# A layer's last additions moved into the scatters: the residual stored to the output early, each expert block's rows added there by DMA

## The chip, the cores and the metric

The kernel runs on one core of one Trainium2 chip. The metric is the time of one execution on the device, in microseconds (us). The kernel before took 378.92 us as the median of 3 runs (378.6 to 380.24). One execution of it was also taken by the hardware profiler; all durations below come from that one.

## The reference

The input is x, 2048 tokens of 128 numbers, float32. Two stages, each with a residual:

```python
x = x + attention(layernorm(x))        # linear "cosformer" attention, 16 heads of 64, then Wo and bo
x = x + moe(layernorm(x))              # mixture of experts, below

logits = xf @ gate_w                   # 8 experts
top_w, top_idx = top_k(logits, 2)      # two experts for each token
top_w = softmax(top_w)
h = gelu(einsum('td,edf->tef', xf, w1) + b1)      # 128 -> 512, exact gelu
y = einsum('tef,efd->ted', h, w2) + b2            # 512 -> 128
out = einsum('ted,te->td', y, combine)            # the two chosen experts' rows, weighed and added
```

So each row of the output is the residual after attention plus two weighed expert results.

## The kernel before

The tokens are worked through in four stages of 512 (`NS = 4`, each of `SC = 4` tiles of 128). In the attention part TensorE (PE) has nearly all of the time. While stage i is in attention, the tokens of stage i-1 are normalised, gated and sent, twice each (once for each of their two experts), by GpSimd's indirect DMAs (`rows_out`) into `ybuf`, a table in DRAM that is sorted by expert. A row of `ybuf` holds the 128 normalised numbers, then a word with the place where the result is to go (column D, copied from `ids`), then the weight (column D + 1). Places that no token took hold 0xFFFF as their word, which is over the scatter's bound, so that such a row is skipped.

The mixture is then computed in `NB = 39` blocks of 128 rows of `ybuf`, each of one expert. A table `tab` says of each block its expert and where it begins. Its first 17 entries are known when three stages are routed (blocks that are already full, sorted by expert), the other 22 at the end (again sorted by expert; entries that are left over point at an empty block). The blocks run as a pipeline over the engines, in this order in each engine's own program:

- SyncE (SP), `load_block(b)`: reads the table, loads the rows into `yb` (a ring of 10) and the expert's first matrix into `w1b` (a ring of 6). From block 10 on it first waits until the scatter of block b-10 has landed (`z_out`), since the scatter reads its row numbers from `yb`.
- PE: transposes the rows (L1324), multiplies by w1 (`hidden`, L1337), then by w2 (`down`, L1352). ScalarE does the gelu (L638).
- VectorE (DVE), `weighed(b)`: adds the bias (`zs`, L986) and multiplies by the weights (`z`, L990, a ring of 8). From block 8 on it waits before L990 until the scatter of block b-8 has landed.
- GpSimd (POOL), `results_out(b)`: one indirect DMA writes the block's 128 rows to `zbuf` (L511). `zbuf` has 2 x 2048 rows, one half for each of a token's two experts, so that no two scatters ever write the same row and none waits for another. The scatters of blocks 0 to 13 are issued in an order written out by hand (`RESULTS_AT`): blocks 0 and 1 after `z` of block 2, block 2 after that of block 3, then four `rows_out`, blocks 3 and 4 after `z` of block 7, block 5 after block 8, 6 and 7 after 9, 8 after 10, 9 and 10 after 11, 11 after 12, and 12 and 13 after 13. From block 14 each waits for its own `z`.

When all 39 scatters have landed, SP and ScalarE's queue load both halves of `zbuf` back (`zin`, eight transfers of 256 KB), DVE adds them to the residual in `x_sb` (`add_results`, L997 and L999), and four stores write the output.

Of the kernel before, what the change touches and what calls it, by code (L numbers as in the profile page):

```python
# [36 lines left out]
SC = 4  # L37
# [63 lines left out]
def moe_block(nc, x, Wq, bq, Wk, bk, Wv, bv, Wo, bo, gate_w, w1, b1, w2, b2,  # L101
              c_rot, c_pair, c_ident, c_small, c_tri, c_ids, out, ybuf, zbuf):
    with ExitStack() as ctx:
# [70 lines left out]
        tab = sb("tab", [1, 2, NB], I32)  # L174
        yb = [sb(f"yb{k}", [P, ROW]) for k in range(3)]
# [3 lines left out]
        b1t = sb("b1t", [P, XR, FB])  # L179
        zs = sb("zs", [P, 2, D])  # L180
# [22 lines left out]
        zin = sb("zin", [P, 2, NC, D])  # L203
# [13 lines left out]
        zin_in = [sem(f"zin_in{k}") for k in range(NS)]  # L217
# [92 lines left out]
        sum_ok = sem("sum_ok")  # L310
        out_ok = sem("out_ok")
# [3 lines left out]
        zv = zbuf.rearrange("(k c p) d -> p k c d", p=P, c=NC)  # L315
        ov = out.rearrange("a (c p) d -> p (a c) d", p=P)
        @block.sync
        def _(sp):
# [52 lines left out]
            def load_block(b):  # L371

                if b >= YR:
                    sp.wait_ge(z_out[(b - YR) % ZR], 16 * ((b - YR) // ZR + 1))
                at = sp.value_load(tab[0:1, 1, b:b + 1], min_val=0, max_val=PLACES)
                sp.dma_start(yb[b % YR][:], ybuf[bass.ds(at, TB), :]).then_inc(yb_in[b % YR], 16)
                if b >= WR:
                    sp.wait_ge(h_ps, 2 * (b - WR) + 2)
                sp.dma_start(w1b[b % WR][:], w1[bass.ds(at // PITCH, 1), :, :].rearrange("e p n -> p (e n)")
                             ).then_inc(w1_in[b % WR], 16)  # L380

            def unit_landed(u):
                sp.wait_ge(y_out[u], 16 * 2 * len(UNITS[u][1]))

            for u in range(TABLES[0] + 1):
                unit_landed(u)
# [4 lines left out]
            for b in range(2, FIRST[1]):  # L391
                load_block(b)
            sp.wait_ge(tab_ok, 2)
# [4 lines left out]

            for k in range(ZR):
                sp.wait_ge(z_out[k], 16 * len(range(k, NB, ZR)))  # L400
            for k in range(NS):
                sp.dma_start(zin[:, 0, k * SC:(k + 1) * SC, :], zv[:, 0, k * SC:(k + 1) * SC, :]).then_inc(zin_in[k], 16)
            for k in (1, 3):
                sp.wait_ge(out_ok, k + 1)
                sp.dma_start(ov[:, k * SC:(k + 1) * SC, :], acc[:, k * SC:(k + 1) * SC, :]).then_inc(stored, 16)
            sp.wait_ge(stored, 16 * NS)

        @block.gpsimd
        def _(pool):
# [97 lines left out]

            def results_out(b):
                if b >= PACED:
                    pool.wait_ge(z_ok, b + 1)  # L510
                pool.indirect_dma_start(zbuf, bass.IndirectOffsetOnAxis(ap=yb[b % YR][:, D:D + 1].bitcast(U32), axis=0),  # L511
                                        z[:, b % ZR, :], None, bounds_check=2 * T - 1, oob_is_err=False).then_inc(z_out[b % ZR], 16)
# [19 lines left out]
        def _(act):  # L532
# [123 lines left out]
            for k in range(ZR):  # L656
                act.wait_ge(z_out[k], 16 * len(range(k, NB, ZR)))
            for k in range(NS):
                act.dma_start(zin[:, 1, k * SC:(k + 1) * SC, :], zv[:, 1, k * SC:(k + 1) * SC, :]).then_inc(zin_in[k], 16)
            for k in (0, 2):  # L660
                act.wait_ge(out_ok, k + 1)
                act.dma_start(ov[:, k * SC:(k + 1) * SC, :], acc[:, k * SC:(k + 1) * SC, :]).then_inc(stored, 16)

        @block.vector
        def _(dve):
# [226 lines left out]
            def table(t, bank=7):  # L892

                n, at = COUNT[t], FIRST[t]
                dve.wait_ge(tab_ps, t + 1)
                dve.tensor_copy(tab[:, 0, at:at + n], ps[0:1, bank, 256:256 + n])
                dve.tensor_scalar(tab[:, 1, at:at + n], ps[0:1, bank, 288:288 + n], float(PLACES), None, ALU.add
                                  ).then_inc(tab_ok, 1)

# [71 lines left out]

            def first_rows():
                expert_of(0)
                expert_of(1)
                dve.wait_ge(xT_ps, NS + 1)
                dve.tensor_copy(xb[:, 0:2, :], ps[:, 6, 0:2 * P].rearrange("p (b r) -> p b r", b=2)).then_inc(xb_ok, 2)

            def block_rows(b):
                expert_of(b)
                dve.wait_ge(xb_ps, b - 1)  # L980
                dve.tensor_copy(xb[:, b % XR, :], ps[:, 5, b % 2 * P:b % 2 * P + P]).then_inc(xb_ok, 1)

# [9 lines left out]

            def add_results(k):

                dve.wait_ge(zin_in[k], 32)
                tile = acc[:, k * SC:(k + 1) * SC, :]
                dve.tensor_tensor(tile, tile, zin[:, 0, k * SC:(k + 1) * SC, :], ALU.add).then_inc(sum_ok, 1)  # L997
                dve.wait_ge(sum_ok, k + 1)
                dve.tensor_tensor(tile, tile, zin[:, 1, k * SC:(k + 1) * SC, :], ALU.add).then_inc(out_ok, 1)  # L999
# [39 lines left out]
            for k in range(NS):  # L1039
                add_results(k)  # L1040
# [356 lines left out]
def shape_constants():  # L1397
# [24 lines left out]
    ids = (np.arange(P)[:, None, None] + P * np.arange(NC)[None, None, :] + T * np.arange(2)[None, :, None])  # L1422
# [33 lines left out]
```

## Time and profile before

| | us |
|---|---|
| median of 3 runs | 378.92 |
| lowest, highest | 378.6, 380.24 |
| span of the profiled execution | 389.7 |
| profiled execution over the median | 10.8 |
| last scatter issued by GpSimd | 373.90 |
| first reload of `zbuf` issued | 376.13 |
| last instruction | 389.7 |

The page gives no own time of the profiled execution other than its span. It is 2.8% over the median: the profiled execution is a slower one, and differences between its places are what is used below. PE is busy in 92% of the span, DVE in 62%, GpSimd in 33%. The three parts of the span are attention (to about 282 us), the blocks (PE's work for them ends at 372 us) and the end, in which no engine but DVE computes.

### The profile page before, as it was taken

The page shows a single profiled execution, that of the slowest core. Times are in us where ns is not written, and L with a number is a line of the kernel's source. Part 1 is how long each engine was busy: PE and PEld are TensorE (multiplying, and loading weights), DVE is VectorE, ACT ScalarE, POOL GpSimd, SP SyncE. Part 2 cuts the span into 40 slices and gives each one's busy share as a digit, 9 for nine tenths or more (in the row PEclk, how much of TensorE's full clock was granted, in tenths as well). Part 3 has the DMA queues.
Part 4 walks back from the last instruction along what each step waited for, and adds up shares of the span by engine and source line. Part 5 has one row for each costly group of instructions (what it writes and reads, how often), then busy time and mean ns, then how long its engine had stood idle before and what let it go on. Part 6 is the DMA issues. An engine that isn't in the chain of part 4 may idle for free.

```text
span 389.7 us, 10955 instructions
## 1 busy us (share of the span) xinstructions
PE 358.1 (92%) x4125; PEld 323.4 (83%) x4125; DVE 241.4 (62%) x735; ACT 156.7 (40%) x369; POOL 129.8 (33%) x130
## 2 busy tenths in 40 slices
PE   8999999999999999999999999999978887999910
PEld 7777999888988988898998889898978777999910
DVE  4889664778756477875647787766545424444415
ACT  3773322565122256512225651222443434555500
POOL 4022511121285112028511302443265454444420
PEclk9999999999999999999999999999998989999985
DMA  7932432330001000000100007004625256876229
GB/s 252 332 156 84 177 130 96 156 129 2 16 31 33 16 2 1 0 19 31 41 8 3 0 14 219 24 19 115 179 93 144 81 166 179 234 203 188 63 81 248
DMA packets 32771, 38.64 MB, mean 99 GB/s; under 512 B 4139, under 2 KB 25024, under 8 KB 31696
## 3 DMA queue, kind: packets, MB, share of 16 engines
q1 hardware_dynamic: 27248, 31.90, 26.4%
q0 software_dynamic: 2272, 4.46, 3.3%
q10 hardware_dynamic: 3200, 1.58, 1.5%
q8 instruction: 34, 0.56, 0.6%
q14 instruction: 17, 0.14, 0.1%
HBM read 22.91 MB, written 15.47 MB: 98 GB/s over the span
## 4 chain that ended last, share of the span: by engine, by line
PE 79%; DVE 7%; DMA 4%; issue 4%; POOL 2%; another core or an unknown queue 1%; ACT 1%; DVEq 1%; SPq 1%; ACTq 0%; POOLq 0%
PE ps L1166 8%; PE ps L1352 8%; PE ps L1128 8%; PE ps L1173 7%; PE ps L1337 7%; PE ps L1145 7%; PE ps L1202 7%; PE ps L1047 5%; PE ps L1049 5%; PE ps L1048 5%; PE ps L1193 4%; PE ps L1092 3%; DMA zin<-zbuf 2%; PE ps L1297 2%; PE ps L1324 1%
## 5 line engine op out<-in xcount | busy, mean ns | idle before, releaser
L597 ACT ACTIVATE os<-ps 128x260 f32<-128x260 f32 x64 | 24.8, 388 | 103.4 <-PE ps L1173 103.3
L638 ACT ACTIVATE hT<-ps,b1t 128x128 f32<-128x128 f32 x156 | 44.9, 368 | 47.9 <-PE ps L1337 26.7
L473 POOL DMA_INDIRECT ybuf<-yr,slot x32 | 31.8, 994 | 75.3 <-DVE yr L845 32.8
L431 POOL TENSOR_TENSOR on<-tcs,rden 128x1024 f32<-128x1024 f32 x16 | 30.4, 1901 | 64.4 <-DVE rden L773 64.4
L511 POOL DMA_INDIRECT zbuf<-z,yb x39 | 37.9, 972 | 39.0 <-DVE z L990 22.3
L760 DVE TENSOR_TENSOR state<-ps,state 128x260 f32<-128x260 f32 x64 | 27.3, 427 | 35.5 <-ACT os L597 29.3
L1352 PE MATMUL ps<-w_sb,hT 128*128 x312 | 43.4, 284 | 3.5 <-DVE zs L986 3.3
L750 DVE TENSOR_TENSOR am<-ps,pair 128x1024 f32<-128x1024 f32 x32 | 38.7, 1208 | 10.0 <-issue 7.5
L1337 PE MATMUL ps<-xb,w1b 128*128 128x128 f32 x312 | 43.9, 286 | 0.0
L1352 PEld LDWEIGHTS ps<-w_sb,hT 128*128 128x128 f32 x312 | 39.3, 198 | 4.3 <-issue 4.2
L1166 PE MATMUL ps<-vcs,am 128*64 128x65 f32 x1024 | 42.5, 225 | 0.2 <-issue 0.2
L1166 PEld LDWEIGHTS ps<-vcs,am 128*64 128x64 f32 x1024 | 36.8, 137 | 3.9
L1337 PEld LDWEIGHTS ps<-xb,w1b 128*128 128x128 f32 x312 | 39.7, 199 | 0.0
L1173 PE MATMUL ps<-vcs,kn 128*64 128x130 f32 x512 | 39.6, 275 | 0.0
L1128 PE MATMUL ps<-qT,kT 64*128 64x128 f32 x512 | 38.0, 285 | 1.0 <-DVE am L750 0.9
L1128 PEld LDWEIGHTS ps<-qT,kT 64*128 64x128 f32 x512 | 31.7, 187 | 7.3 <-issue 6.6
L1145 PE MATMUL ps<-state,qT 64*128 64x130 f32 x480 | 34.8, 279 | 0.5 <-DVE tcs L766 0.4
L715 DVE TENSOR_SCALAR vcs<-os,cs 128x512 f32<-128x512 f32 x64 | 32.6, 551 | 1.1
L1145 PEld LDWEIGHTS ps<-state,qT 64*128 64x128 f32 x480 | 30.2, 187 | 2.5 <-DVE tcs L766 1.4
L1202 PE MATMUL ps<-wo_sb,oT 128*128 128x128 f32 x256 | 31.6, 278 | 0.0
L1202 PEld LDWEIGHTS ps<-wo_sb,oT 128*128 128x128 f32 x256 | 29.8, 192 | 1.7 <-issue 1.4
L711 DVE TENSOR_TENSOR os<-ps,bv_all 128x512 f32<-128x512 f32 x32 | 22.0, 689 | 14.7 <-PE ps L1049 14.7
(120 smaller groups left out, 585.7 us busy)
## 6 DMA issues: line engine op xcount, KB each, us to landing
w1b<-in_L_ffn_w SPq DMA_DIRECT2D x39, 256.0 KB
ybuf<-blank SPq DMA_DIRECT2D x8, 1152.0 KB, 4.7
yb<-ybuf SPq DMA_DIRECT2D x39, 72.0 KB
w_sb<-in_L_ffn_w SPq DMA_DIRECT2D x8, 256.0 KB
x_sb<-in_L_attn_x SPq DMA_DIRECT2D x4, 256.0 KB, 5.4
pair<-c_pair SPq DMA_DIRECT2D x16, 64.0 KB, 2.4
zin<-zbuf SPq DMA_DIRECT2D x4, 256.0 KB, 5.5
zin<-zbuf ACTq DMA_DIRECT2D x4, 256.0 KB, 6.0
```

The costliest lines, as they stand in the source:

```text
L473: pool.indirect_dma_start(ybuf, bass.IndirectOffsetOnAxis(ap=slot[:, k, c:c + 1], axis=0), yr[:, k, c, :], None).then_inc(y_out[u], 16)
L511: pool.indirect_dma_start(zbuf, bass.IndirectOffsetOnAxis(ap=yb[b % YR][:, D:D + 1].bitcast(U32), axis=0), z[:, b % ZR, :], None, bounds_c ...
L638: act.activation(hT[:, b % 2, f, :], ps[:, b % 2 * 2 + f // 2, f % 2 * P:f % 2 * P + P], ACT.Gelu, bias=b1t[:, b % XR, f:f + 1]).then_inc( ...
L715: last = dve.tensor_scalar(vcs[:, m // 2, (m % 2) * 8:(m % 2) * 8 + 8, s, 0:DH], vb[:, m % 2, :].rearrange("p (h d) -> p h d", d=DH), cs4[ ...
L750: dve.tensor_tensor(am[:, p % 2, :, :, :], ps[:, 0:2, :].rearrange("p r (q t) -> p r q t", t=P), pair[:, c, None, None, :].broadcast_to([P ...
L1128: last = mm(ps[:, r, b * P:(b + 1) * P], kT[rows, of, c * P:(c + 1) * P], qT[rows, of, c * P:(c + 1) * P], start=True, stop=True)
L1145: mm(ps[:, 2 + 2 * (n % 2) + r, 0:2 * CS].rearrange("p (s b v) -> p b s v", s=2, b=2)[:, q, :, :], qT[rows, 2 * g + q, c * P:(c + 1) * P], ...
L1166: mm(ps[t:t + 64, 2 + 2 * (n % 2) + r, q * VW:q * VW + VW], am[:, n // 2 % 2, r, (2 * g + q) % (PH // 2), t:t + 64], vcs[:, c, g * GH + 2 ...
L1173: last = mm(ps[64 * r:64 * r + 64, 2 + 2 * (n % 2) + q, 2 * CS:3 * CS], kn[:, c, (2 * g + q) * P + r * DH:(2 * g + q) * P + (r + 1) * DH], ...
L1202: last = mm(ps[:, 7, at:at + D], oT[:, c % 2, pr, :], wo_sb[:, pr, :], start=(pr == 0), stop=(pr == NP - 1))
L1337: last = mm(ps[:, b % 2 * 2 + f // 2, f % 2 * P:f % 2 * P + P], w1b[b % WR][:, f * P:(f + 1) * P], xb[:, b % XR, :], start=True, stop=True ...
L1352: last = mm(ps[:, z_bank(b), 0:D], hT[:, b % 2, f, :], w, start=(f == 0), stop=(f == FB - 1))
```

## The change

`zbuf` and `zin` are gone. SP stores the residual of each stage from `x_sb` to `out` (`residual_out`): stages 0 to 2 ahead of the first block load, stage 3 after the load of block 5. `results_out(b)` now scatters to `out` itself, with `compute_op=ALU.add`: the DMA reads the row of the output, adds the block's row and writes the sum. Row numbers are token numbers (`ids` holds each of them twice), copied by DVE from `yb` into `tokens`, so that `yb` is free when `z` is computed and `load_block` waits for `z_ok` in place of `z_out`. The end of SP's program waits for the stores and the scatters; ScalarE's and DVE's parts of the end are gone.

A token's two results can now stand in two blocks that add to the same row. Two additions to one row must not be under way together, so the scatters wait for each other: block 0 for the four stores, blocks 1 to 8 for the landing of the block ahead, and from block 9 on every block for the landing of block b-2, and for that of b-1 if the two are of different experts. DVE computes that from the table: `turn[b]` is 16 where the expert changes and 0 where it doesn't, and GpSimd loads it into a register and waits on it.

```diff
@@ sync: load_block, residual_out and the end
                 if b >= YR:
-                    sp.wait_ge(z_out[(b - YR) % ZR], 16 * ((b - YR) // ZR + 1))
+                    sp.wait_ge(z_ok, b - YR + 1)
...
+            def residual_out(i):
+
+                sp.wait_ge(x2_ok, (i + 1) * SC)
+                sp.dma_start(ov[:, i * SC:(i + 1) * SC, :], acc[:, i * SC:(i + 1) * SC, :]).then_inc(stored, 16)
...
+            for i in range(NS - 1):
+                residual_out(i)
...
             for b in range(2, FIRST[1]):
                 load_block(b)
+                if b == 5:
+                    residual_out(NS - 1)
...
+            sp.wait_ge(stored, 16 * NS)
             for k in range(ZR):
                 sp.wait_ge(z_out[k], 16 * len(range(k, NB, ZR)))
-            for k in range(NS):
-                sp.dma_start(zin[:, 0, k * SC:(k + 1) * SC, :], zv[:, 0, k * SC:(k + 1) * SC, :]).then_inc(zin_in[k], 16)
-            for k in (1, 3):
-                sp.wait_ge(out_ok, k + 1)
-                sp.dma_start(ov[:, k * SC:(k + 1) * SC, :], acc[:, k * SC:(k + 1) * SC, :]).then_inc(stored, 16)
-            sp.wait_ge(stored, 16 * NS)
@@ gpsimd: results_out
+            def landed(b, count):
+
+                pool.wait_ge(z_out[b % ZR], count)
+
             def results_out(b):
+                if b == FIRST[1]:
+                    pool.wait_ge(turn_ok, 2)
+                if b > ZR:
+                    other = pool.value_load(turn[0:1, b:b + 1], min_val=0, max_val=16)
                 if b >= PACED:
                     pool.wait_ge(z_ok, b + 1)
-                pool.indirect_dma_start(zbuf, bass.IndirectOffsetOnAxis(ap=yb[b % YR][:, D:D + 1].bitcast(U32), axis=0),
-                                        z[:, b % ZR, :], None, bounds_check=2 * T - 1, oob_is_err=False).then_inc(z_out[b % ZR], 16)
+                if b == 0:
+                    pool.wait_ge(stored, 16 * NS)
+                if 1 <= b <= ZR:
+                    landed(b - 1, 16)
+                if b > ZR:
+                    landed(b - 1, other + 16 * ((b - 1) // ZR))
+                    pool.tensor_tensor(after[:, b:b + 1], neg_half[:, 0:1], neg_half[:, 0:1], ALU.add)
+                    landed(b - 2, 16 * ((b - 2) // ZR + 1))
+                pool.indirect_dma_start(rows, bass.IndirectOffsetOnAxis(ap=tokens[:, b:b + 1], axis=0),
+                                        z[:, b % ZR, :], None, bounds_check=T - 1, oob_is_err=False, compute_op=ALU.add).then_inc(z_out[b % ZR], 16)
@@ scalar: the end
-            for k in range(ZR):
-                act.wait_ge(z_out[k], 16 * len(range(k, NB, ZR)))
-            for k in range(NS):
-                act.dma_start(zin[:, 1, k * SC:(k + 1) * SC, :], zv[:, 1, k * SC:(k + 1) * SC, :]).then_inc(zin_in[k], 16)
-            for k in (0, 2):
-                act.wait_ge(out_ok, k + 1)
-                act.dma_start(ov[:, k * SC:(k + 1) * SC, :], acc[:, k * SC:(k + 1) * SC, :]).then_inc(stored, 16)
@@ vector: table, block_rows (first_rows likewise), the end
+                dve.wait_ge(tab_ok, t + 1)
+                later = slice(max(at, 1), at + n)
+                dve.tensor_tensor(turn[:, later], tab[:, 0, later], tab[:, 0, later.start - 1:later.stop - 1],
+                                  ALU.not_equal).then_inc(turn_ne, 1)
+                dve.wait_ge(turn_ne, t + 1)
+                dve.tensor_scalar(turn[:, later], turn[:, later], 16, None, ALU.mult).then_inc(turn_ok, 1)
...
+            def tokens_of(b):
+                dve.tensor_copy(tokens[:, b:b + 1], yb[b % YR][:, D:D + 1].bitcast(U32))
...
                 dve.tensor_copy(xb[:, b % XR, :], ps[:, 5, b % 2 * P:b % 2 * P + P]).then_inc(xb_ok, 1)
+                tokens_of(b)
...
-            for k in range(NS):
-                add_results(k)
```

On GpSimd, from the scatter of block 0 to that of block 10, the program before reads as follows; L511 is the scatter of a block, L473 the last stage's `rows_out`, and what an instruction waits for stands in brackets.

```order
L511 DMA zbuf<-z,yb 4096x128 [waits z_ok]
L511 DMA zbuf<-z,yb 4096x128
L511 DMA zbuf<-z,yb 4096x128 [waits z_ok]
L473 DMA ybuf<-yr,slot 30848x144 [waits slot_ok,wts_ok,rows_ok,z_ok]
L473 DMA ybuf<-yr,slot 30848x144
L473 DMA ybuf<-yr,slot 30848x144 [waits z_ok] x2
L511 DMA zbuf<-z,yb 4096x128 [waits z_ok]
L511 DMA zbuf<-z,yb 4096x128
L511 DMA zbuf<-z,yb 4096x128 [waits z_ok] x2
L511 DMA zbuf<-z,yb 4096x128
```

The changed program at the same place: L533 is the scatter, L479 `rows_out`, `z_out3` the landing of block 3 (the number is the block's modulo 8). The last rows are block 9 and, but for its scatter, block 10.

```order
L533 DMA out<-z,tokens 2048x128 [waits z_out2,z_ok]
L533 DMA out<-z,tokens 2048x128 [waits z_out3]
L533 DMA out<-z,tokens 2048x128 [waits z_out4,z_ok]
L533 DMA out<-z,tokens 2048x128 [waits z_out5,z_ok]
L533 DMA out<-z,tokens 2048x128 [waits z_out6]
L533 DMA out<-z,tokens 2048x128 [waits z_out7,z_ok]
L522 TENSOR_LOAD turn [waits z_ok]
L522 ISA x2
L516 REGISTER_ALU
L531 TENSOR_TENSOR after<-neg_half 128x1 [waits z_out0]
L533 DMA out<-z,tokens 2048x128 [waits z_out7]
```

A scatter that had no wait, or one for `z` alone, now stands behind the landing of the scatter ahead of it; from block 9 a load, register work and a small addition stand ahead of each.

At the end of SP's program, before, stand the last block's loads, then the reloads and stores:

```order
L379 DMA w1b<-in_L_ffn_w 128x512
L402 DMA zin<-zbuf 128x4x128 [waits z_out4,z_out5,z_out3,z_out6,z_out2,z_out7,z_out1,z_out0]
L402 DMA zin<-zbuf 128x4x128 x3
L405 DMA out<-x_sb 128x4x128 [waits out_ok] x2
L103 UNCONDITIONAL_BRANCH [waits stored]
```

and in the changed program the branch that ends it comes right behind the loads:

```order
L377 TENSOR_LOAD tab [waits z_ok]
L377 ISA x2
L378 ISA
L378 DMA yb<-ybuf 128x144
L381 ISA [waits h_ps]
L381 DMA w1b<-in_L_ffn_w 128x512
L103 UNCONDITIONAL_BRANCH [waits z_out4,z_out3,z_out5,z_out2,z_out6,z_out1,z_out7,z_out0,stored]
```

Nothing is left of the end but the wait for the last landings.

## Rows read from the trace of the kernel before

**Rows 1.** The page's head and engines' busy time.
```profile
span 389.7 us, 10955 instructions
PE 358.1 (92%) x4125; PEld 323.4 (83%) x4125; DVE 241.4 (62%) x735; ACT 156.7 (40%) x369; POOL 129.8 (33%) x130
```

**Rows 2.** Windows: stretch, its length, engines' busy time, PE clock, DMA share, GB/s.
```profile
340.00:360.00 20.00, 19.94 (x171) 19.37 (x171) 9.50 (x41) 11.26 (x41) 9.69 (x10) 1.00 0.71 200
...
376.00:390.00 14.00, 0.00 (x0) 0.00 (x0) 5.54 (x8) 0.00 (x0) 0.00 (x0) 0.52 0.83 225
```

**Rows 3.** The chain that ended last: start, length, what.
```profile
373.90 2.08 DMA zbuf<-z,yb
...
377.75 7.81 DMA zin<-zbuf
385.58 0.70 DVE x_sb L997
386.31 0.69 DVE x_sb L999
```

**Rows 4.** Sequencer instructions of the program's end: count, ns min/median/max, first and last start.
```profile
L103 POOLq DRAIN  x1: 7075/7075/7075, 373.7 to 373.7; - x1
...
L103 SPq COMPARE_BRANCH  x1: 41/41/41, 389.3 to 389.3; - x1
```

**Rows 5.** GpSimd's timeline: start, length, instruction, idle before and what ended it.
```profile
289.14 0.20 POOL L459 COPY yr<-ids 128x4 uint32<-128x4 uint32 x1
...
291.55 1.00 POOL L511 DMA_INDIRECT zbuf<-z,yb  x1 [1.89 <-DVE z L990]
...
297.57 0.96 POOL L473 DMA_INDIRECT ybuf<-yr,slot  x1 [1.95 <-DVE yr L845]
298.84 0.96 POOL L473 DMA_INDIRECT ybuf<-yr,slot  x1 [0.30 <-issue]
...
305.18 0.98 POOL L511 DMA_INDIRECT zbuf<-z,yb  x1 [1.29 <-DVE z L990]
306.47 0.98 POOL L511 DMA_INDIRECT zbuf<-z,yb  x1 [0.30 <-issue]
...
311.15 0.97 POOL L511 DMA_INDIRECT zbuf<-z,yb  x1 [2.43 <-DVE z L990]
...
313.70 0.97 POOL L511 DMA_INDIRECT zbuf<-z,yb  x1 [0.30 <-issue]
...
342.69 0.97 POOL L511 DMA_INDIRECT zbuf<-z,yb  x1 [0.93 <-issue]
...
364.75 0.97 POOL L511 DMA_INDIRECT zbuf<-z,yb  x1 [0.93 <-DVE z L990]
...
373.90 0.97 POOL L511 DMA_INDIRECT zbuf<-z,yb  x1 [0.35 <-issue]
```

**Rows 6.** DVE's timeline: stage 3's last residual, weighings of blocks 11 and 38.
```profile
281.32 0.29 DVE L778 TENSOR_TENSOR x_sb<-ps,x_sb 128x128 f32<-128x128 f32 x1 [2.05 <-PE ps L1202]
...
315.63 0.29 DVE L986 TENSOR_TENSOR zs<-ps,b_all 128x128 f32<-128x128 f32 x1 [2.98 <-PE ps L1352]
...
372.84 0.28 DVE L990 TENSOR_SCALAR z<-zs,yb 128x128 f32<-128x128 f32 x1
```

**Rows 7.** SP's timeline: the load of block 16's rows.
```profile
315.79 0.34 SPq L376 DMA_DIRECT2D yb<-ybuf  x1
```

**Rows 8.** SP's table loads: count, ns min/median/max.
```profile
L375 SPq TENSOR_LOAD <-tab x39: 4/268/467, 265.0 to 358.2; - x39
L375 SPq FUSED_REGOPS  x39: 3/152/181, 265.5 to 358.5; - x39
```

**Rows 9.** DMA issues: queue, count, size, median us from issue to landing.
```profile
pair<-c_pair SPq DMA_DIRECT2D x16, 64.0 KB, 2.4
out<-x_sb ACTq DMA_DIRECT2D x2, 256.0 KB, 3.5
```

**Rows 10.** DVE's small copy of each block, and what it waited for.
```profile
L970 DVE COPY b1t<-b_all x39: 165/170/276, 269.9 to 368.4; 128x4 f32 x39
```

More of the change, by code:

```diff
@@ L101, in moe_block @@
 def moe_block(nc, x, Wq, bq, Wk, bk, Wv, bv, Wo, bo, gate_w, w1, b1, w2, b2,
-              c_rot, c_pair, c_ident, c_small, c_tri, c_ids, out, ybuf, zbuf):
+              c_rot, c_pair, c_ident, c_small, c_tri, c_ids, out, ybuf):
     with ExitStack() as ctx:
@@ L174, in moe_block @@
         tab = sb("tab", [1, 2, NB], I32)
+        turn = sb("turn", [1, NB], I32)
+        after = sb("after", [P, NB])
         yb = [sb(f"yb{k}", [P, ROW]) for k in range(3)]
@@ L179, in moe_block @@
         b1t = sb("b1t", [P, XR, FB])
+        tokens = sb("tokens", [P, NB], U32)
         zs = sb("zs", [P, 2, D])
@@ L202, in moe_block @@
         w1b += [sb(f"w1b{k}", [P, F]) for k in range(2, WR)]
-        zin = sb("zin", [P, 2, NC, D])
+        sb("under_qT", [P, NP, ST])
         hT = sb("hT", [P, 2, FB, P])
@@ L216, in moe_block @@
         z_out = [sem(f"z_out{k}") for k in range(ZR)]
-        zin_in = [sem(f"zin_in{k}") for k in range(NS)]
         tri_in = sem("tri_in")
@@ L309, in moe_block @@
         z_ok = sem("z_ok")
-        sum_ok = sem("sum_ok")
-        out_ok = sem("out_ok")
+        turn_ne = sem("turn_ne")
+        turn_ok = sem("turn_ok")
         block = ctx.enter_context(nc.Block())
         f32 = lambda ap: ap.bitcast(F32)
-        zv = zbuf.rearrange("(k c p) d -> p k c d", p=P, c=NC)
+        rows = out.rearrange("a t d -> (a t) d")
         ov = out.rearrange("a (c p) d -> p (a c) d", p=P)
@@ L975, in first_rows @@
                 dve.wait_ge(xT_ps, NS + 1)
+                tokens_of(0)
+                tokens_of(1)
                 dve.tensor_copy(xb[:, 0:2, :], ps[:, 6, 0:2 * P].rearrange("p (b r) -> p b r", b=2)).then_inc(xb_ok, 2)
@@ L991, in weighed @@
                                   ).then_inc(z_ok, 1)
[L993 to L999, printed above, removed]
             first_rows()
@@ L1421, in shape_constants @@
     tri = np.stack([np.triu(np.ones((P, P)), 1), np.ones((P, P))], axis=1).astype(np.float32)
-    ids = (np.arange(P)[:, None, None] + P * np.arange(NC)[None, None, :] + T * np.arange(2)[None, :, None])
+    ids = np.repeat(np.arange(P)[:, None, None] + P * np.arange(NC)[None, None, :], 2, axis=1)
     return {"c_rot": rot, "c_pair": pair, "c_ident": np.eye(P, dtype=np.float32), "c_small": small,
@@ L1451 @@
     ybuf = nc.dram_tensor("ybuf", (PLACES + TB, ROW), F32).ap()
-    zbuf = nc.dram_tensor("zbuf", (2 * T, D), F32).ap()
-    moe_block(nc, *args, out, ybuf, zbuf)
+    moe_block(nc, *args, out, ybuf)
     r = run_bass_kernel_spmd(nc, [arrays], core_ids=[0])
```

## The prediction

> **What bounds the kernel now.** I read the page's head first: PE has 92% of the span [rows 1]. The windows say where that is not so: from 340 to 360 us PE is busy 19.94 of 20 us, and from 376 on it does nothing while the DMA engines are 83% busy [rows 2]. So there are two bounds: PE while there are blocks, and the end behind it. The chain of waits names the end: the last scatter, started at 373.90, lands 2.08 us later, then come 7.81 us of reloads and DVE's last additions [rows 3]. From the landing at 375.98 to 389.7 that is 13.7 us, and this is what the change takes away.
>
> Then I read GpSimd's timeline, since the new waits stand there. Its scatters have no waits for each other: those of blocks 3 and 4 start 1.28 us apart (305.18 and 306.47, block numbers counted from 291.55 as block 0), and from block 22 (342.69) to block 33 (364.75) eleven steps take 22.06 us, 2.0 us each, which is PE's pace [rows 5]. GpSimd is busy 0.97 us of that. In all, blocks 3 to 38 take 373.90 - 305.18 = 68.7 us, 35 steps of 1.96 us. That number is what the new chain must not exceed.
>
> **The end.** Removed: 13.7 us. What is late next? SP's program now ends with the last landing, but so does GpSimd's, and its DRAIN took 7.075 us from 373.7 [rows 4], to 380.8, which is 6.9 us after the last scatter's start. Before, the reloads covered it. I take it as the price of ending behind a scatter: 6.9 us, and 0.4 for the last barrier (389.3 to 389.7) [rows 4], 7.3 from the last scatter's start to the end. The other bound is that the drain isn't needed there: the landing and 0.4. Before, that stretch was 389.7 - 373.9 = 15.8. So the end gains 8.5 us by the drain, and 13.3 by a plain landing.
>
> **The stores.** Stages 0 to 2 go out while SP has nothing to load. Stage 3's waits for the residual that ends at 281.61 [rows 6]; a store of this size landed in 3.5 us [rows 9], so by about 286, and the scatter of block 0 starts at 291.55 [rows 5]. Covered, by 5 us. Behind it SP has the loads of blocks 6 to 9; they move a few us later, but are needed by PE one by one from about 292. I cost this at nothing; without cover it would be 2 or 3 us, once.
>
> **DVE.** Added: 39 copies of one column, at 0.17 us each as its other small copy [rows 10], and four tiny operations for `turn`. DVE is 9.5 us busy in 20 [rows 2], so they fall into its idle time: nothing. Removed beside the end: nothing.
>
> **SP's wait.** `load_block` waits for `z_ok` in place of `z_out`, so loads come earlier. The waits of about 3 us in DVE's row of block 11 [rows 6] might shrink with it, or with GpSimd's bursts of three scatters, which end. Worth up to some us on PE, but only if PE is still what the end waits for.
>
> **The new chain.** How many steps of each kind? Blocks 1 to 8 each wait for the landing of the one ahead. From 9 on only a change of expert does so. Counting the router's choices on the reference's own inputs gives experts 0 0 1 1 2 2 2 3 3 4 4 5 5 5 6 6 7 for the first table and 0 0 1 1 2 2 2 3 3 4 4 5 5 6 6 7 7 7 7 and three empty blocks for the second: changes at 9, 11, 14, 16, 17, 19, 21, 24, 26, 28, 30, 32 and 36. So of the 35 steps from block 3 to 38, 5 + 13 = 18 wait for the landing ahead, and 17 don't. Where two of the 17 stand in a row (blocks 13, 23, 34 and 38 are second ones) the wait for b-2 makes both together last at least one landing step.
>
> A landing step S is the landing L, from the DMA's start, and GpSimd's answer. The answer: `z` of block 38 ends at 373.12 [rows 6] and its scatter starts at 373.90 [rows 5], 0.78 us; with a part of the small addition I take 0.85. L: the trace has no accumulating DMA. From below it is the plain scatter with idle DMA engines, 2.08 us [rows 3]. Under load a plain one took longer: block 6's started at 311.15 [rows 5], and the load that waits for it was issued at 315.79 [rows 7], behind 0.42 us of table work [rows 8], so at most 4.2 us. From above: the plain scatter and, in series, a read of 64 KB from DRAM, which took 2.4 us [rows 9], 4.5 us. I take 3.2, near the middle: most of the steps stand beside weight loads (71% DMA share [rows 2]) and each now reads first. S = 4.05.
>
> A free step P: 1.28 us as blocks 3 to 4 [rows 5], and the addition, 0.2 us as GpSimd's small copy (at 289.14) [rows 5], with a little for its start: 1.6. Table load and registers (0.42 us on SP [rows 8]) I take as covered by the running DMA instruction; if not, P is 2.2. Without any of it 1.3.
>
> **The sum.** Block 0 at 291.55 [rows 5]. Two steps of S to block 2. Then four `rows_out`, 1.27 us apart (297.57 to 298.84) [rows 5], and block 3: 6.4 us. So block 3 at 291.55 + 8.1 + 6.4 = 306.05 (before 305.18). Then 18 x 4.05 = 72.9, 17 x 1.6 = 27.2, and for the four second ones 4 x (4.05 - 3.2) = 3.4: block 38 starts at 409.6. The end 7.3: 416.9, against 389.7, so +27.2. Steps average 2.96 us against PE's 2.0, so PE is not the bound: `z` of block b waits for the landing of block b-8, DVE holds PE back, and what PE or the loads gain or lose is hidden. On the median of the runs: 378.92 + 27.2 = 406.1. The profiled span is 10.8 us over that median; if what it adds are stalls of PE, the chain doesn't lose them and the change costs more, if it is in landings, less.
>
> **A rule weighed.** The trace shows 2.08 us for the plain landing [rows 3]. The Trainium skill, "DMA: Bandwidth & Descriptors", section "Latency and other measured facts", gives an access to HBM 0.2 us on average and 2 us at high load. If an accumulate paid one such access more, an estimate from that page would be L = 2.28 or 4.08, and by the same sum a result near 385 or 427.
>
> **The rivals.**
> - *The read is nearly free, the end's saving wins (faster).* Place: the landings of blocks 4 to 38 on GpSimd. With L = 2.08 block 3 stays at 305.18; 18 x 2.93 + 27.2 puts block 38 at 385.1, and with the plain landing behind it (2.5) the end at 387.6, -2.1: 376.8 (P = 1.4: 373). It decides at L = 2.19 with that end; with the drain at 1.93, which no row shows. For it: the last scatters' 2.08 us. Against: the loads beside it until late, and the bound of 4.2 us under load [rows 5, 7].
> - *A small price.* L = 2.3, drain at the end: 305.2 + 56.7 + 27.2 + 7.3 = 396.4, +6.7: 385.6.
> - *Heavier issue.* An accumulate names two reads for each row, so GpSimd's 0.97 us could grow, to double at most. With half of it, S = 4.55 and P = 2.1: 307.1 + 81.9 + 35.7 + 1.4 + 7.8 = 433.9, +44: 423. No row speaks for or against.
> - *The scatters keep up with PE.* The steps would have to average 1.96 us, S at most 2.3, so L 1.45. Then the end alone counts, -8.5: 370. Every landing in the rows is longer.
> - *`turn` doesn't spare anything,* each step waits: 306.05 + 35 x 4.05 + 7.3 = 455.1, +65: 444.
>
> **How the numbers follow.** Forecast 0.57; heavier issue 0.13; small price 0.09; nearly free 0.12; keeps up 0.03; between small price and free, no change that can be measured, 0.04; `turn` 0.02. Faster by over 0.5% (which is about what a measurement of this kernel can tell from no change): 0.15, within 0.05, slower 0.80. The likeliest case's own range is 390 to 425 (L from 2.5 to 4). For 8 in 10 I take 378 to 430: below lies most of "nearly free", above part of the heavier issue and the upper bounds (L = 4.5 and P = 2.2: 442).
>
> **What would show it.** In the changed profile: GpSimd's scatters some 4 us apart where the expert changes and 1.6 where not; DVE's L990 waiting for scatters from about block 16; PE busy well under 90% behind 320 us; the last scatter near 409, a drain of about 7 us behind it; the chain of waits made of scatters and GpSimd in place of PE. The forecast is wrong if the accumulating scatter lands in 2.2 us beside loads, if GpSimd follows PE's 2.0 us, or if its own 0.97 us is another number.

## The result: 427.25 us, and the profile after

The changed kernel took 427.25 us (median of 4 runs, 424.42 to 429.01) against 379.58 us for the kernel before (4 runs on the same chip, 378.6 to 380.35). The ratio is 1.1248, with a 95% interval of 1.121 to 1.1286: slower, as forecast, and by more than the 406.1 us that were named: inside the range of 378 to 430, near its upper end, and over the 425 that the likeliest case had been given.

The page's head and engine line of the changed kernel, in the form of [rows 1]:

```profile
span 424.8 us, 11133 instructions
PE 359.3 (85%) x4125; PEld 324.5 (76%) x4125; DVE 238.1 (56%) x770; ACT 156.7 (37%) x369; POOL 159.3 (37%) x160
```

PE has the same work as before and a smaller share of a longer span. GpSimd is 29.5 us busier, with 30 instructions more. Its indirect DMAs are where most of that comes from; the page's group, and the two groups of the DMA issues and of DVE's weighing:

```profile
L533 POOL DMA_INDIRECT out<-z,tokens x39 | 60.6, 1554 | 33.7 <-DMA out<-z,tokens 14.7
...
L1017 DVE TENSOR_SCALAR z<-zs,yb 128x128 f32<-128x128 f32 x39 | 11.8, 302 | 55.0 <-DMA out<-z,tokens 54.0
...
out<-z,tokens POOLq DMA_INDIRECT x39, 3.3
```

The adding scatter occupies GpSimd for 1554 ns, the plain one 0.97 us [rows 5]; it lands 3.3 us after its issue (the last number, a median). It also goes out in another form. The pages' lines of GpSimd's DMA queue (packets, MB, share of the DMA engines), before and after:

```profile
q0 software_dynamic: 2272, 4.46, 3.3%
q0 software_dynamic: 6640, 4.47, 6.9%
```

The bytes are the same, but there are 4368 packets more, 112 for each of the 39 scatters. In the trace a plain scatter of 128 rows is 16 packets of 4 KB and 16 small ones, an adding one 128 packets, one for each row (512 B, or 8 B where the row is skipped), and 16 small ones.

DVE stands 54.0 us in front of its weighing for a slot of `z`, so for the landing of the scatter eight blocks back. The waits behind 290 us (engine, operand and line, what was waited for: us in total, times, longest) show the whole chain of who holds whom:

```profile
DVE z L1017 <- DMA out<-z,tokens: 54.0, 24, 3.8
PEld ps L1341 <- issue: 34.1, 22, 3.7
PE ps L1341 <- DVE xb L1007: 30.5, 22, 3.5
POOL after L531 <- DMA out<-z,tokens: 26.7, 13, 3.7
POOL out L533 <- DMA out<-z,tokens: 14.7, 5, 4.5
```

GpSimd waits for landings, DVE for the same landings, PE for DVE. (The 13 + 5 waits of GpSimd in the list are not the 18 landing steps of the forecast one by one: the list has the first two steps and a second free step among them, and puts three others down to DVE, as below.) The windows, columns as in [rows 2], give what is left of PE:

```profile
300.00:320.00 20.00, 12.97 (x94) 12.40 (x93) 4.97 (x26) 6.43 (x22) 9.50 (x8) 0.90 0.52 129
320.00:390.00 70.00, 47.28 (x350) 44.37 (x350) 20.21 (x105) 23.59 (x83) 36.81 (x40) 0.93 0.49 100
390.00:417.00 27.00, 4.97 (x41) 4.55 (x40) 2.33 (x10) 2.28 (x8) 17.96 (x21) 0.65 0.20 17
417.00:425.00 8.00, 0.00 (x0) 0.00 (x0) 0.00 (x0) 0.00 (x0) 1.55 (x1) 0.50 0.02 0
```

Where [rows 2] had 19.94 of 20 us, PE is busy for 68% (47.28 of 70), and from 390 to 417 us, when its work is nearly done, GpSimd is still sending scatters. The granted clock falls from 0.93 to 0.65 there, between the levels 2.4 GHz (1.00) and 1.2 GHz (0.50), as PE idles; its last matmul ends at 395.07, and nothing waits for PE by then.

GpSimd's timeline, first where the chain begins, then its last stretch (start, length, instruction, idle before and what ended it), which answers [rows 5]:

```profile
304.48 1.60 POOL L533 DMA_INDIRECT out<-z,tokens  x1 [0.30 <-issue]
308.51 1.55 POOL L533 DMA_INDIRECT out<-z,tokens  x1 [2.44 <-DMA out<-z,tokens]
313.03 1.54 POOL L533 DMA_INDIRECT out<-z,tokens  x1 [2.96 <-DVE z L1017]
318.02 1.54 POOL L533 DMA_INDIRECT out<-z,tokens  x1 [3.44 <-DVE z L1017]
...
397.10 1.55 POOL L533 DMA_INDIRECT out<-z,tokens  x1 [0.52 <-issue]
398.12 0.76 POOL L531 TENSOR_TENSOR after<-neg_half 128x1 f32<-128x1 f32 x1
399.04 1.55 POOL L533 DMA_INDIRECT out<-z,tokens  x1 [0.16 <-issue]
402.22 0.18 POOL L531 TENSOR_TENSOR after<-neg_half 128x1 f32<-128x1 f32 x1 [1.63 <-DMA out<-z,tokens]
402.92 1.55 POOL L533 DMA_INDIRECT out<-z,tokens  x1 [0.52 <-issue]
...
417.10 1.55 POOL L533 DMA_INDIRECT out<-z,tokens  x1 [0.16 <-issue]
```

From 397.10 to 399.04 is a step inside an expert, 1.94 us: the small addition begins 1.02 us into the running scatter, takes 0.76, and the next scatter follows 0.16 us behind it. From 399.04 to 402.92 is a change of expert, 3.88 us: the landing and its answer. The step from 308.51 is named a wait for DVE; the `z` that it needs, block 8's, was done before 300 us, and the landing of the scatter ahead came last.

The drain of GpSimd's program, as in [rows 4]:

```profile
L103 POOLq DRAIN  x1: 8062/8062/8062, 416.5 to 416.5; - x1
```

It ends at 424.6, 7.5 us behind the last scatter's start; to the end of the span are 7.7 us.

### The profile page after: what moved, and what is told of

The parts are those of the page before. It is cut to its first block, busy times and chain, and to the rows that moved or that the text cites. A ratio compares the mean times of both kernels' runs of the same rounds, so it can differ in the third digit from the quotient of the medians.

```text
span 424.8 us, 11133 instructions
## 1 busy us (share of the span) xinstructions
PE 359.3 (85%) x4125; PEld 324.5 (76%) x4125; DVE 238.1 (56%) x770; ACT 156.7 (37%) x369; POOL 159.3 (37%) x160
## 4 chain that ended last, share of the span: by engine, by line
PE 57%; issue 15%; DMA 10%; POOL 8%; DVE 4%; POOLq 3%; SPq 1%; ACT 0%; DVEq 0%
DMA out<-z,tokens 8%; PE ps L1145 8%; PE ps L1183 8%; PE ps L1162 6%; PE ps L1190 6%; PE ps L1219 6%; PE ps L1064 5%; PE ps L1066 5%; PE ps L1065 5%; POOL out L533 4%; PE ps L1210 3%; PE ps L1109 3%; POOLq L522 2%; POOL ybuf L479 2%; POOL after L531 2%
## 5 line engine op out<-in xcount | busy, mean ns | idle before, releaser
L533 POOL DMA_INDIRECT out<-z,tokens x39 | 60.6, 1554 | 33.7 <-DMA out<-z,tokens 14.7
L479 POOL DMA_INDIRECT ybuf<-yr,slot x32 | 31.9, 996 | 68.9 <-DVE yr L860 31.0
L1369 PE MATMUL ps<-w_sb,hT 128*128 x312 | 45.0, 291 | 0.6 <-DVE zs L1013 0.5
L1354 PE MATMUL ps<-xb,w1b 128*128 128x128 f32 x312 | 45.5, 292 | 0.0
L775 DVE TENSOR_TENSOR state<-ps,state 128x260 f32<-128x260 f32 x64 | 27.4, 428 | 31.8 <-ACT os L619 29.5
L1017 DVE TENSOR_SCALAR z<-zs,yb 128x128 f32<-128x128 f32 x39 | 11.8, 302 | 55.0 <-DMA out<-z,tokens 54.0
L1369 PEld LDWEIGHTS ps<-w_sb,hT 128*128 128x128 f32 x312 | 41.2, 206 | 1.1 <-issue 1.1
L1341 PE MATMUL ps<-ident,yb 128*128 128x128 f32 x37 | 11.3, 304 | 30.6 <-DVE xb L1007 30.5
L1162 PE MATMUL ps<-state,qT 64*128 64x130 f32 x480 | 33.3, 277 | 0.0
L1341 PEld LDWEIGHTS ps<-ident,yb 128*128 128x128 f32 x37 | 5.4, 146 | 34.4 <-issue 34.3
```

The lines of the kernel that those rows point to most:

```text
L479: pool.indirect_dma_start(ybuf, bass.IndirectOffsetOnAxis(ap=slot[:, k, c:c + 1], axis=0), yr[:, k, c, :], None).then_inc(y_out[u], 16)
L533: pool.indirect_dma_start(rows, bass.IndirectOffsetOnAxis(ap=tokens[:, b:b + 1], axis=0), z[:, b % ZR, :], None, bounds_check=T - 1, oob_i ...
L1162: mm(ps[:, 2 + 2 * (n % 2) + r, 0:2 * CS].rearrange("p (s b v) -> p b s v", s=2, b=2)[:, q, :, :], qT[rows, 2 * g + q, c * P:(c + 1) * P], ...
L1354: last = mm(ps[:, b % 2 * 2 + f // 2, f % 2 * P:f % 2 * P + P], w1b[b % WR][:, f * P:(f + 1) * P], xb[:, b % XR, :], start=True, stop=True ...
L1369: last = mm(ps[:, z_bank(b), 0:D], hT[:, b % 2, f, :], w, start=(f == 0), stop=(f == FB - 1))
```

## The experiments

All compare with the kernel before on the same chip. "Chain" is GpSimd's timeline from the scatter of block 3 to that of block 38, "end" what follows to the end of the span.

**The end alone.** The changed kernel, with plain scatters that wait for nothing but their `z`, into a buffer that nobody reads:

```diff
-                if b > ZR:
-                    landed(b - 1, other + 16 * ((b - 1) // ZR))
-                    pool.tensor_tensor(after[:, b:b + 1], ...)
-                    landed(b - 2, 16 * ((b - 2) // ZR + 1))
-                pool.indirect_dma_start(rows, ..., compute_op=ALU.add).then_inc(z_out[b % ZR], 16)
+                pool.indirect_dma_start(zbuf, ...).then_inc(z_out[b % ZR], 16)
```

> The changed kernel with plain scatters into a buffer of their own (two halves, as before) and without any wait of one scatter for another; the residual is stored early and nothing is reloaded or added, so the output lacks the mixture. What is left of the change is the end. Chain theory (the landings that GpSimd waits for make the loss): 368 to 372 us; the 15.8 us behind the last scatter become 7.3 if GpSimd's drain of 7 us is needed there, 2.5 if not (366). Rival (the loss is in the early stores, the copies, the loads' new order): over 400 us.

Measured: 369.44 us, ratio 0.9732 [0.9661, 0.9803]. The span is 367.1 us, the last scatter starts at 360.02, the end is 7.1 us. GpSimd's drain, behind a plain scatter as well:

```profile
L103 POOLq DRAIN  x1: 7235/7235/7235, 359.6 to 359.6; - x1
```

So the end's saving is real, 15.8 us are now 7.1, and its other bound (only a landing) is out: the 7 us drain had been hidden behind the reloads. The loss is not in the early stores, the copies or the new order of the loads, all of which this kernel has. Part of its gain over the kernel before is the loads' (see "Only the loads' wait").

**The addition without the waits.** The same kernel, with the scatters adding:

```diff
-                                        z[:, b % ZR, :], None, bounds_check=2 * T - 1, oob_is_err=False)
+                                        z[:, b % ZR, :], None, bounds_check=2 * T - 1, oob_is_err=False, compute_op=ALU.add)
```

> As the run with the end alone, but the scatters add (compute_op) to the two halves, still without waits for each other; the output lacks the mixture. Chain theory: an accumulating scatter holds GpSimd 1.55 us, under PE's 2.0 us a block, so it costs 1 to 5 us over the end alone, by the scatters that GpSimd starts late: 371 to 377 us. Rival (the accumulating scatter itself is what costs, by GpSimd's time and the DMA engines'): most of the 48 us are here, over 400 us.

Measured: 371.56 us, ratio 0.979 [0.9723, 0.9857]; 2.1 us over the one above. From GpSimd's timeline, and the tile view of the buffer:

```profile
343.15 1.54 POOL L517 DMA_INDIRECT zbuf<-z,tokens  x1 [0.30 <-issue]
345.00 1.54 POOL L517 DMA_INDIRECT zbuf<-z,tokens  x1 [0.30 <-issue]
```

```profile
L517 POOL DMA_INDIRECT zbuf<-z,tokens x39: 1544/1544/1620, 286.1 to 361.6; - x39
...
DMA to landing us min/median/max: 2.7/4.7/5.9
```

GpSimd sends them back to back, every one from block 3 on 1.85 us behind the one ahead, just inside PE's 2.0. The plain ones needed only 1.28 and so caught up with PE sooner; the last one starts 1.6 us later here (361.64 against 360.02), which is most of the 2.1. The longer instruction is there without any wait, so it comes with the addition. The landings are long (a median of 4.7 us of the 19 that the trace tells), and nobody minds.

**The waits without the addition.** The changed kernel, its scatters plain:

```diff
-                                        z[:, b % ZR, :], None, bounds_check=T - 1, oob_is_err=False, compute_op=ALU.add)
+                                        z[:, b % ZR, :], None, bounds_check=T - 1, oob_is_err=False)
```

> The changed kernel with all its waits, but plain scatters onto the output instead of adding ones (each row keeps the last written). Chain theory: a landing step falls from about 4.3 to about 3.6 us (landing 2.8 in place of 3.5), a free step from 1.93 to 1.35: 18 x 0.7 + 17 x 0.6 = 23 us less than the changed kernel, 404 us. Rival (the add is what costs): within 5 us of the run with the end alone, about 375 us.

Measured: 400.82 us, ratio 1.0551 [1.0477, 1.0626]. GpSimd's timeline:

```profile
379.10 0.99 POOL L533 DMA_INDIRECT out<-z,tokens  x1 [0.16 <-issue]
381.35 0.19 POOL L531 TENSOR_TENSOR after<-neg_half 128x1 f32<-128x1 f32 x1 [1.26 <-DMA out<-z,tokens]
382.06 0.99 POOL L533 DMA_INDIRECT out<-z,tokens  x1 [0.53 <-issue]
383.08 0.21 POOL L531 TENSOR_TENSOR after<-neg_half 128x1 f32<-128x1 f32 x1
383.45 0.99 POOL L533 DMA_INDIRECT out<-z,tokens  x1 [0.16 <-issue]
```

A free step is 1.39 us (382.06 to 383.45), a landing step 2.96 here and 3.60 as a mean of the 18: near the 404 us expected, far from the rival's 375. Against the end alone, the four kernels make a square:

| us | plain | adding | the addition costs |
|---|---|---|---|
| no waits | 369.44 | 371.56 | 2.1 |
| waits | 400.82 | 427.25 | 26.4 |
| the waits cost | 31.4 | 55.7 | |

(427.25 comes from other runs than the rest; the kernel before took 0.6 us more beside them.) The upper row also writes to another buffer and has no table loads or small additions; these stand in the free step, 1.39 us with them and 1.28 without. The waits make the change slower with nothing added. The addition costs nearly nothing where scatters are only sent, and 24.3 us more (26.4 less 2.1) with the waits. Not all of that is waiting for landings. From block 3 to 38 the adding kernel takes 112.6 us and the plain one 90.9: 12.8 of the difference are in the 18 landing steps, but 8.9 in the 17 free ones, in which only the second ones wait for a landing. There it is the longer instruction, which was hidden while PE set the pace and shows now that GpSimd does.

**Every scatter waits for the landing ahead.** The counts are constants, so table load and small addition go:

```diff
-                if b > ZR:
-                    other = pool.value_load(turn[0:1, b:b + 1], min_val=0, max_val=16)
...
-                    landed(b - 1, other + 16 * ((b - 1) // ZR))
-                    pool.tensor_tensor(after[:, b:b + 1], ...)
-                    landed(b - 2, 16 * ((b - 2) // ZR + 1))
+                    landed(b - 1, 16 * ((b - 1) // ZR + 1))
```

> The changed kernel in which every scatter waits for the landing of the one ahead, by a constant; no register load, no small addition. Chain theory: the 17 free steps of 1.93 us become landing steps of about 4.0, 35 x 4.0 = 140 us from block 3 to 38 in place of 112.6: 450 to 460 us. Rival (the register loads and the small additions on GpSimd are the price): faster than the changed kernel, under 420 us.

Measured: 459.2 us (456.64 to 462.57), ratio 1.2124 [1.2015, 1.2233]; the last steps on GpSimd's timeline:

```profile
436.06 1.54 POOL L529 DMA_INDIRECT out<-z,tokens  x1 [2.63 <-DMA out<-z,tokens]
440.10 1.54 POOL L529 DMA_INDIRECT out<-z,tokens  x1 [2.50 <-DMA out<-z,tokens]
443.63 1.54 POOL L529 DMA_INDIRECT out<-z,tokens  x1 [1.98 <-DMA out<-z,tokens]
447.15 1.54 POOL L529 DMA_INDIRECT out<-z,tokens  x1 [1.98 <-DMA out<-z,tokens]
```

35 steps took 142.5 us (304.67 to 447.15), 4.07 us each: 3.25 of landing and 0.82 of answer. That is near the step S of the forecast (4.05). The rival in the prediction in which every step waits had its chain end at 455.1; the span is 454.8. And `turn` spares 459.2 - 427.25 = 32 us. By the steps it should be 17 x (4.07 - 2.05) = 34.3, less 18 x (4.32 - 4.07) = 4.5, as the landing steps were the longer ones where free steps stood between: 29.8.

**Are the loads what makes landings long?** The changed kernel without the loads of `w1` from block 6 on:

```diff
                 if b >= WR:
                     sp.wait_ge(h_ps, 2 * (b - WR) + 2)
-                sp.dma_start(w1b[b % WR][:], w1[...]).then_inc(w1_in[b % WR], 16)
+                else:
+                    sp.dma_start(w1b[b % WR][:], w1[...]).then_inc(w1_in[b % WR], 16)
...
-                pe.wait_ge(w1_in[b % WR], 16 * (b // WR) + 16)
+                pe.wait_ge(w1_in[b % WR], 16)
```

> The changed kernel without the loads of w1 from block 6 on (33 of 39; the blocks use what their buffer held, so the output is another). It measures how much of a landing step is the company of the loads. Theory (load): landings fall from 3.3 to 4.3 us to about 2.7 as the last three have, so the 18 landing steps from 4.32 to 3.55 on average: 14 us less, 413 us. Rival (the read and the write are slow by themselves): 423 to 427 us.

Measured: 419.26 us, ratio 1.1043 [1.1016, 1.107], 8 us under the changed kernel, between the two expectations. The bytes did go: from 320 to 390 us the DMA engines' share is 0.28 and 37 GB/s, against 0.49 and 100 above.

```profile
320.00:390.00 70.00, 51.87 (x383) 49.00 (x382) 21.97 (x112) 25.48 (x88) 40.45 (x44) 0.91 0.28 37
```

Landing steps fell from 4.32 to 4.05 us and the mean landing from 3.47 to 3.25. So the loads add some 0.2 to 0.3 us to a landing.

The expectation had put the floor at 2.7 us, "as the last three have". Those three are blocks 36 to 38, the empty ones: every row of theirs is skipped. The windows of the changed kernel show it (the last number is GB/s), first the stretch of blocks 32 and 33, then all of blocks 36 to 38:

```profile
402.00:408.00 6.00, 0.00 (x0) 0.00 (x0) 0.00 (x0) 0.00 (x0) 4.46 (x6) 0.50 0.26 23
413.00:425.00 12.00, 0.00 (x0) 0.00 (x0) 0.00 (x0) 0.00 (x0) 5.12 (x5) 0.50 0.02 0
```

The last load of a block is issued at 378.04, so blocks 30 to 35 tell what an adding scatter with rows takes beside no loads. The view of the scatters of blocks 26 to 34, then of blocks 36 to 38:

```profile
L533 POOL DMA_INDIRECT out<-z,tokens x9: 1550/1550/1552, 385.2 to 407.3; - x9
DMA to landing us min/median/max: 3.1/3.3/3.6
L533 POOL DMA_INDIRECT out<-z,tokens x3: 1550/1552/1552, 413.2 to 417.1; - x3
DMA to landing us min/median/max: 2.7/2.7/2.7
```

The kernel in which every scatter waits shows it by rows, since there no two scatters overlap and its last loads are issued at 385.24 (blocks 24 to 38; a row that moves is a packet of 512 B in the trace):

| rows of the block that move | 0 | 10 | 39 | 71 | 91 | 99 | 128 (seven blocks) |
|---|---|---|---|---|---|---|---|
| issue to landing, us | 2.68 to 2.70 | 2.89 | 3.13 | 3.11 | 3.22 | 3.21 | 3.27 to 3.48 |

So a landing with most rows takes 3.1 to 3.6 us, and not 2.7, with no load beside it, and the mean of 3.25 without the `w1` loads is near that: the second expectation, that the read and the write are slow by themselves, gave the better reason. In the kernel with waits and plain scatters blocks 30 to 35 land in 2.24 us on average and the empty three in 2.11. The addition adds 0.6 us to an empty scatter, which is its longer instruction, and 1.05 to one of blocks 30 to 35; the other 0.5 come with the rows that are moved.

**The kernel before again,** profiled once more, since its profiled execution (a span of 389.7) stood 2.8% over the median of its runs:

> The kernel before once more, for a second profile of it. Its first profiled execution had a span of 389.7 us against a median of 378.9, while the four kernels with early stores had spans 1 to 4 us under their medians. Theory: that execution had extra stalls of PE between 286 and 328 us, and a second one has them again (span near 390). Rival: it was one slow execution; a second has a span near 377.

Measured: 379.87 us, a span of 378.1. Two windows over the same stretch, of the execution shown ahead of the prediction and of this one:

```profile
300.00:350.00 50.00, 43.61 (x358) 42.02 (x357) 19.68 (x84) 23.48 (x83) 24.26 (x25) 0.97 0.61 175
```

```profile
300.00:350.00 50.00, 46.68 (x395) 44.97 (x395) 22.38 (x93) 26.30 (x92) 25.90 (x27) 1.00 0.71 203
```

The last scatters start 11.7 us apart (373.90 and 362.24). All of it is time of PE: for the same 4125 matmuls it was busy 358.1 us in the first [rows 1] and 351.4 in the second, 6.7 more, and it stood idle for the other 5. DVE's waits of 3 us for PE as in [rows 6] are gone (the longest is 1.6). What is left of waits for `yb`:

```profile
PEld ps L1324 <- DMA yb<-ybuf: 3.1, 3, 1.7
PE ps L1324 <- DMA yb<-ybuf: 2.4, 2, 1.6
```

**Only the loads' wait.** The kernel before, end and all, with `tokens` copied and `load_block` waiting for `z_ok`:

```diff
-                    sp.wait_ge(z_out[(b - YR) % ZR], 16 * ((b - YR) // ZR + 1))
+                    sp.wait_ge(z_ok, b - YR + 1)
...
-                pool.indirect_dma_start(zbuf, bass.IndirectOffsetOnAxis(ap=yb[b % YR][:, D:D + 1].bitcast(U32), axis=0),
+                pool.indirect_dma_start(zbuf, bass.IndirectOffsetOnAxis(ap=tokens[:, b:b + 1], axis=0),
```

> The kernel before with one part of the change alone: DVE copies the row numbers into tokens, and the loads of blocks from 10 on wait for z_ok in place of the scatter's landing. Plain scatters into their own buffer, whole end. Theory (loads were never late enough to count without the profiler): 378 to 380 us, same. Rival (late loads stall PE between 286 and 328 us): 368 to 374 us. The run with the end alone had this part in it and saved 9.5 us, of which the end accounts for 8.7.

Measured over 10 runs: 376.33 us, ratio 0.9943 [0.992, 0.9966]. That lies between the two expectations. The waits for `yb` are gone from the list, and PE is busier in the same window:

```profile
300.00:350.00 50.00, 49.41 (x422) 48.14 (x421) 24.77 (x124) 28.54 (x100) 26.92 (x29) 1.00 0.67 187
```

The last scatter starts at 358.51 in place of 362.24. This is the part of the change that pays by itself, 2.6 us, and the fastest version found with the mixture in its output. The end alone is then worth 376.33 - 369.44 = 6.9 us more, which no version with the mixture in it reached.

**Can the reloads be made shorter instead?** Two ways. First the buffer's rows side by side, so that a partition's four rows are one piece of 2 KB where they were four of 512 B, in the kernel before and in the last one:

```diff
-        zv = zbuf.rearrange("(k c p) d -> p k c d", p=P, c=NC)
+        zv = zbuf.rearrange("(k p c) d -> p k c d", p=P, c=NC)
...
-    ids = (np.arange(P)[:, None, None] + P * np.arange(NC)[None, None, :] + T * np.arange(2)[None, :, None])
+    ids = (NC * np.arange(P)[:, None, None] + np.arange(NC)[None, None, :] + T * np.arange(2)[None, :, None])
```

> The kernel before, but the row of token c x 128 + p in the result buffer is 16 p + c, so that a reload reads 2 KB side by side per partition in place of four pieces of 512 B. If the reloads are bound by the small pieces (2 MB in 9.4 us): 2 to 3 us faster, 376 us. If they are bound by DRAM or by their issue: same, 379 us.

> Both: rows side by side in the result buffer, and loads that wait for z_ok. Expected the sum of the two single effects: 375 to 377 us if the loads don't count, under 372 if they do.

Measured: 378.97 us, ratio 1.0005 [0.9986, 1.0024], and 377.77 us, 0.9969 [0.9946, 0.9993]. No gain, and behind the loads' wait, if anything, a loss (377.77 against 376.33; the intervals overlap). From the last scatter's start to the end are 15.9 and 16.1 us, against 15.8 and 14.9 in the kernels with the old pieces. The chain's rows of the last reload, in pairs of old and new pieces: the kernel before (second profile) and side by side, then the same two with the loads' wait:

```profile
366.09 7.81 DMA zin<-zbuf
363.34 7.27 DMA zin<-zbuf
```

```profile
362.37 6.85 DMA zin<-zbuf
362.27 7.42 DMA zin<-zbuf
```

One pair goes one way and one the other. The number of pieces isn't what the reload takes its time for; what it is, is open.

Second, parts of 5, 5, 4 and 2 tiles in place of four each, so that less stands behind the last landing (6 runs):

```diff
+ENDS = (slice(0, 5), slice(5, 10), slice(10, 14), slice(14, 16))
...
-                sp.dma_start(zin[:, 0, k * SC:(k + 1) * SC, :], zv[:, 0, k * SC:(k + 1) * SC, :]).then_inc(zin_in[k], 16)
+                sp.dma_start(zin[:, 0, ENDS[k], :], zv[:, 0, ENDS[k], :]).then_inc(zin_in[k], 16)
```

> The kernel before with the loads that wait for z_ok (376.3 us alone), and the end in parts of 5, 5, 4 and 2 tiles in place of four of 4, so that the last additions and the last store are half as long. Reloads bound the end, so the last landing stays; behind it 0.7 us of additions and some 0.3 us of store go: 375.3 us. Rival (the end is bound by the sum of loads and stores that share the DMA engines): 376.3 us.

Measured: 376.69 us, ratio 0.9925 [0.9906, 0.9944]. The kernel without it had 376.33 and 0.9943 [0.992, 0.9966] on another chip; the ratios differ by 0.002, some 0.7 us, and their intervals overlap, so no gain is shown.

## Why the prediction was right in its sign and short in its size

| step of the forecast | forecast | measured |
|---|---|---|
| block 3 starts | 306.05 | 304.48 |
| landing step S, 18 of them | 4.05 | 4.32 (77.7 in all) |
| free step P, 17, with the second ones' 3.4 | 1.8 (30.6 in all) | 2.05 (34.9 in all) |
| end behind the last scatter | 7.3 | 7.7 |
| end of the span | 416.9 | 424.8 |
| rise over the profiled execution before | +27.2 | +35.1, or +46.7 over the second one |

**The mechanism** was as named: 18 landing steps and 17 free ones on GpSimd, DVE behind them, PE no longer the bound, and a drain in place of the reloads. The square shows it by runs: the waits make it slower by 31.4 us with nothing added.

**The end.** Removed 15.8, left 7.3: the end alone has 7.1 and the changed kernel 7.7. Right; the bound without a drain is refuted by every kernel here that ends so.

**The stores** were covered. They landed 4.2 us after issue, so stage 3's by 282, and the first scatter started at 286.00. The first two landing steps were long, 5.48 and 6.04 us (286.00, 291.48, 297.52), where 4.05 was assumed, so that block 3 came only 1.6 us sooner than forecast though block 0 began 5.5 us sooner than in [rows 5]. Why these landings took 4.70 and 5.22 us is open: from 286 to 291 us the DMA engines' share was 0.89, but without most of the `w1` loads, at a share of 0.27, they still took 4.03 and 5.06.

**S was short by 0.27,** 4.8 us in all. The landings that the 18 steps wait for took 3.53 us on average where L was 3.2 (3.47 over all of blocks 3 to 38), and the answer 0.79 where 0.85 was assumed. The plain scatter's 3.60 in the same place shows that 0.72 of the step is the addition's. That L came near is in part luck. It was put near the middle of two bounds, and the lower one, 2.08 us for "the plain scatter with idle DMA engines" [rows 3], is the landing of block 38, an empty block whose rows are all skipped; the prediction counts the three empty blocks but doesn't draw on that. A plain one with rows lands in 2.24 us there, so the bound itself moves little. But the same 2.08 is what stood for the rival "nearly free".

**P was the mis-sized term.** "1.28 us as blocks 3 to 4, and the addition, 0.2" took the DMA instruction's 0.97 us as given. It is 1.55, and the step inside an expert 1.94 where the plain one has 1.39; the 17 make 33.0 us where 27.2 were forecast. The prediction had named this as one of its signs of being wrong ("if its own 0.97 us is another number"), and the rival "heavier issue" had that part right (its P was 2.1; its S of 4.55 was too long). The table load was covered, as assumed: with the small addition it costs the plain step 0.1 us (1.39 against 1.28), where 0.3 had been put. The second ones cost 1.9 us and not 3.4: blocks 13, 23 and 34 were late by 0.1, 1.3 and 0.5, and at block 38 two steps of 1.94 outlast the landing of an empty block. Together +4.3 us.

These make -1.6 + 4.8 + 4.3 + 0.4 = 7.9 us, the distance of the spans. **The larger part of the miss was the base.** The sum was made on a span of 389.7 and its rise put on a median of 378.92, 10.8 us lower. That assumes that the changed kernel loses the same 10.8, and the prediction said when it wouldn't: "if what it adds are stalls of PE, the chain doesn't lose them". They were PE's time, 5 us of stalls and 6.7 of slower work; the second profile lacks them, and the changed kernel's end is set by GpSimd's chain, whose first scatter started at 286.00 like the second profile's (286.44) and not at 291.55. The remaining 2.45 us lie between the profiled span (424.8) and the median (427.25): 1.8 is what a run's time has over its span, 0.6 the median over the profiled run. In all 7.9 + 10.8 + 2.45 = 21.15, the whole of 427.25 - 406.1. Taken from the chain's own end the forecast would have been 416.9 and the 1.8 us around a span, 418.7.

**SP's wait** was put at "up to some us", hidden while GpSimd is the bound. It is worth 2.6 us by itself; in the changed kernel, where PE is busy two thirds of the time, it should not show, but no run takes it out there.

**The rule weighed.** The Trainium skill's "DMA: Bandwidth & Descriptors", section "Latency and other measured facts", has 0.2 or 2 us for an access to HBM, and the prediction had asked what one such access more would make of the landing. It came out at neither end. In the same kernel the addition lengthened the mean landing from 2.64 to 3.47 us, 0.83, of which the longer instruction is 0.6, as the empty scatters show. What is left is 0.2 on average, and 0.5 for the rows of blocks 30 to 35, beside no loads. No run times one access alone.

## What to carry to other kernels

Before a transfer is put in a chain of waits, multiply its full step (landing and answer, 3.6 to 4.3 us here) by the links, and compare with the bound engine's pace over the same stretch; a saving at the end is paid once, a link every time. An operation that is cheap while another engine sets the pace can be dear once its own engine and its landing do: adding cost 2.1 us in the one case and 26.4 in the other. Before a price is read from a row, make sure that the instruction there does the work in question: the last scatters were the easiest to read, and they moved no row. And where the bound moves to another engine, forecast the new end from its own start and steps; don't carry over a difference from a profiled execution that stands off the median.

## What the runs showed of the hardware

- An indirect DMA of 128 rows of 512 B that adds at its target holds GpSimd for 1.54 to 1.64 us, a plain one for 0.97 to 1.02. The adding one goes out as 128 packets, one for each row, the plain one as 16 of 4 KB (39 scatters: 4368 packets more for the same bytes).
- Beside no loads the adding one landed in 3.1 to 3.6 us, the plain one in 2.2 to 2.3 (blocks 30 to 35). With every row skipped they took 2.7 and 2.1, and the adding one's landing grew with the rows that it moved, to 3.3 to 3.5 at 128. Beside the loads the longest landings were 5.9 us (adding, back to back) and 4.4 (plain).
- A program that ends behind such scatters pays a drain of GpSimd. Its length is from 7.1 to 9.2 us in six kernels, but that is because it starts up to 1.8 us before the last scatter does (359.8 for 361.64 where they had come back to back). Its end lies 6.8 or 6.9 us behind the start of the last scatter where that is plain and 7.4 or 7.5 where it adds.
- A small GpSimd addition (128x1) takes 0.18 to 0.29 us beside nothing or a plain scatter, and 0.74 to 0.77 where it begins inside a running adding scatter; it starts before that instruction's end, 1.02 us into it.
- Reloading 2 MB from DRAM in pieces of 2 KB took as long as in pieces of 512 B (378.97 us against 378.93).
